# Softmax's division moved from the context to the probabilities, in a three-stage transformer kernel

## The reference, cut to what matters

```
scores = einsum('bhqd,bhkd->bhqk', q / sqrt(32), k) + attention_bias      # 8 x 16 x 512 x 512
scores = where(src_mask, -inf, scores)
probs  = softmax(scores, axis=-1)
ctx    = einsum('bhqk,bhkd->bhqd', probs, v)                              # then reshaped to B, S, D
x      = x + (ctx @ Wo + bo)
```

## Time and profile before

| | |
|---|---|
| time, median of 3 runs | 2397.74 us (2396.6 to 2398.53) |
| the profiled execution | 2398.12 us, its span 2396.3 us |
| granted TensorE clock, mean | 0.998 |
| busy: TensorE / VectorE / ScalarE / GpSimd | 2362.5 / 1359.5 / 1012.1 / 1019.7 us |
| attention stage, first score to last turn | 794.3 to 1672 us |

### The profile page before, as it was taken

The page is one execution under the profiler, slowest core; times in us unless marked ns, Lnnn a source line. Parts: engine busy times, 40 slices in busy tenths (PEclk is TensorE's granted clock), DMA queues, the critical chain, the costliest instruction groups (busy, mean ns, idle before and its releaser), DMA issues. The chain is left out here.

```text
span 2396.3 us, 42236 instructions
## 1 busy us (share of the span) xinstructions
PE 2362.5 (99%) x16100; PEld 1894.6 (79%) x16100; DVE 1359.5 (57%) x2749; ACT 1012.1 (42%) x2057; POOL 1019.7 (43%) x829
## 2 busy tenths in 40 slices
PE   9999999999999899999999999997999999999999
PEld 7788888888888677777777777775888888888887
DVE  7355464555557777777777777778443333323332
ACT  6132232331332776776767676767311111111111
POOL 0042341432424896767677776767113203203200
PEclk9999999999999999999999999999999999999999
DMA  7110101101122556565656566564320110110100
GB/s 231 42 45 21 44 24 55 44 18 61 44 73 102 161 182 205 168 200 163 212 158 203 170 200 194 169 211 164 123 71 1 53 53 0 53 53 1 51 35 18
DMA packets 142197, 243.94 MB, mean 102 GB/s; under 512 B 14140, under 2 KB 28620, under 8 KB 142048
## 3 DMA queue, kind: packets, MB, share of 16 engines
q1 hardware_dynamic: 141520, 241.66, 31.4%
q10 hardware_dynamic: 528, 0.26, 0.0%
HBM read 216.69 MB, written 25.20 MB: 101 GB/s over the span
## 5 line engine op out<-in xcount | busy, mean ns | idle before, releaser
L1254 POOL TENSOR_TENSOR at_bias<-at_bias,at_mask 128x512 f32<-128x512 f32 x512 | 596.4, 1192 | 231.7 <-DMA at_bias<-in_fside_Bx16xSxS 224.8
L646 ACT ACTIVATE L_hid<-bank,L_b1c 128x512 f32<-128x512 f32 x256 | 176.6, 690 | 962.0 <-PE bank L290 961.8
L845 DVE CAST L_hh<-L_hid 128x512 fp32r<-128x512 f32 x256 | 122.9, 480 | 739.1 <-PE bank L972 710.5
L288 PE MATMUL bank<-xth,L_w1h 128*128 128x512 f32 x1024 | 403.2, 394 | 0.1
L289 PE MATMUL bank<-xth,L_w1l 128*128 128x512 f32 x1024 | 400.0, 391 | 0.0
L290 PE MATMUL bank<-xtl,L_w1h 128*128 128x512 f32 x1024 | 399.7, 390 | 0.0
L970 PE MATMUL bank<-L_w2h,L_hh 128*128 128x512 f32 x1016 | 398.4, 392 | 0.0
L972 PE MATMUL bank<-L_w2l,L_hh 128*128 128x512 f32 x1016 | 396.0, 390 | 0.0
L971 PE MATMUL bank<-L_w2h,L_hl 128*128 128x512 f32 x1016 | 395.8, 390 | 0.0
L1311 ACT ACTIVATE at_bias<-at_bias,cos_sin 128x512 f32<-128x512 f32 x512 | 363.3, 713 | 8.5 <-DVE cos_sin L1452 8.0
L1452 DVE CUSTOM_DVE_ANT_0 at_bias<-bank,at_bias 128x512 f32<-128x512 f32 x512 | 331.3, 684 | 36.6 <-PE bank L1643 24.6
(11 more groups left out here) (213 smaller groups left out, 3240.9 us busy)
## 6 DMA issues: line engine op xcount, KB each, us to landing
at_bias<-in_fside_Bx16xSxS SPq DMA_DIRECT2D x256, 512.0 KB, 3.7
L_xres<-in_x SPq DMA_DIRECT2D x8, 1024.0 KB, 5.3
x_scratch<-L_xres SPq DMA_DIRECT2D x8, 1024.0 KB, 4.3
at_xres<-x_scratch SPq DMA_DIRECT2D x32, 256.0 KB, 4.3
L_xin<-x_scratch SPq DMA_DIRECT2D x8, 1024.0 KB, 5.6
L_xres<-x_scratch SPq DMA_DIRECT2D x8, 1024.0 KB, 5.6
L_ring<-in_L_cond_w SPq DMA_DIRECT2D x31, 256.0 KB, 4.9
L_xin<-in_x SPq DMA_DIRECT2D x7, 1024.0 KB, 5.2
```

Source lines behind the costliest of these rows:

```text
L288: nc_mm = pe.matmul(out, ah, bh, start=i == 0, stop=False)
L646: nc.scalar.activation(hid[m % 2][:, :], turn[m % 2][:, :], func, bias=b1c[:, m:m + 1]).then_inc(h_act, 1)
L1254: nc.gpsimd.tensor_tensor(tile, tile, mask[:, m % TT, :], ALU.add).then_inc(masked, 1)
```

## The change

The division goes to the probabilities: behind the exponentials of a block, VectorE takes the reciprocals of its four sums and multiplies each of the four units in place by its column (`scale`), and TensorE's turn of a unit waits for that (`scaled`) instead of for the exponential. `over`, `over_by`, `normal` and `normalize` go. The two halves of the context are read from `ctx_ps` itself, and the next phase's context waits for the low half. The copy of unit 1 goes from VectorE to ScalarE. VectorE's `inverse` and scales 0 and 1 stand at the head of its turn, scales 2 and 3 behind scores 0 and 1. Its core (semaphore lists and deleted bodies left out):

```diff
@@ scalar
+            done = pt_odd if j % 2 else pt_even
+            nc.scalar.activation(pt[:, j, :, :].rearrange("p k q -> p (k q)"), turn[j % 2][:, :], ACT.Copy).then_inc(done, 1)
...
         def context_hi(b, phase, alone=False):
-            act.wait_ge(normed, b * PHASES + phase + 1)
+            act.wait_ge(pv_mm, b * BLOCKS + TT * phase + TT)
...
-            nc.scalar.activation(cth[:, phase, :], normal[:, :], ACT.Identity, bias=bvc[:, phase:phase + 1]).then_inc(ct_hi, 1)
+            nc.scalar.activation(cth[:, phase, :], ctx_ps[:, :], ACT.Identity, bias=bvc[:, phase:phase + 1]).then_inc(ct_hi, 1)
...
@@ scalar, body
-                if u == 0 and phase:
-                    over(b, phase - 1, first)
-                elif u == 0 and not first:
-                    over(b - 1, PHASES - 1)
...
+                turn_out(b, m, 1, first)
                 if after:
                     exp(*after, 1)
@@ vector
+        def inverse(b, m):
+
+            dve.wait_ge(exped, b * UNITS + GROUP * m + GROUP)
+            nc.vector.reciprocal(inv[:, 0:GROUP], sums[:, GROUP * m:GROUP * m + GROUP]).then_inc(inv_set, 1)
+            dve.wait_ge(inv_set, b * BLOCKS + m + 1)
+
+        def scale(b, m, j):
+            tile = bias[:, (GROUP * m + j) % SLOTS, :]
+            nc.vector.tensor_scalar(tile, tile, inv[:, j:j + 1], None, ALU.mult).then_inc(scaled, 1)
...
-            nc.vector.scalar_tensor_tensor(ctl[:, phase, :], normal[:, :], bvc[:, phase:phase + 1],
+            nc.vector.scalar_tensor_tensor(ctl[:, phase, :], ctx_ps[:, :], bvc[:, phase:phase + 1],
...
@@ vector, body
                 before = m - 1
+                inverse(b, m)
+                scale(b, m, 0)
+                scale(b, m, 1)
...
                 if after:
                     scores(*after, 0)
+                scale(b, m, 2)
+                if after:
                     scores(*after, 1)
-                if u == 0 and phase:
-                    normalize(b, phase - 1)
-                elif u == 0 and not first:
-                    normalize(b - 1, PHASES - 1)
-                if u == TT - 1:
-                    inverse(b, phase, first)
-                turn_out(b, m, 1, first)
+                scale(b, m, 3)
                 if after:
                     scores(*after, 2)
@@ tensor
-                pe.wait_ge(normed, b * PHASES + tile)
+                pe.wait_ge(ct_lo, b * PHASES + tile)
...
-            pe.wait_ge(exped, b * UNITS + n + 1)
+            pe.wait_ge(scaled, b * UNITS + n + 1)
...
-            if j == 0 and m % TT == 0 and not (first and m == 0):
-                pe.wait_ge(over_out, b * PHASES + m // TT)
...
@@ tensor, body
-                if m % TT == TT - 1:
-                    over(b, m // TT)
```

More of the change, by code:

```diff
@@ L1119, in attention_stage @@
     pt = at(HIDDEN, "pt", [P, GROUP, KT, P])
-    over_by, normal = at(PT, "over_by", [P, S]), at(SETUP, "normal", [P, S])
-    spread = normal[:, :].rearrange("p (n d) -> p n d", d=HD)
     neg_top, sums, inv = keep.neg_top, keep.sums, keep.inv
@@ L1134, in attention_stage @@
         "masked", "score_mm", "scored", "exped", "turned", "pt_even", "pt_odd", "pv_mm"))
[L1135 to L1139, removed]
+    x_mm, nat_mm, v_mm, o_mm = map(sem, ("x_mm", "nat_mm", "v_mm", "o_mm"))
+    xt_hi, xt_lo, nat_hi, nat_lo, v_out, o_out = map(sem, ("xt_hi", "xt_lo", "nat_hi", "nat_lo", "v_out", "o_out"))
+    inv_set, scaled, ct_hi, ct_lo, res_ready = map(sem, ("inv_set", "scaled", "ct_hi", "ct_lo", "res_ready"))
     passed_dve, passed_sp = sem("passed_dve"), sem("passed_sp")
@@ L1405, in scalar @@
         each_pair(act, body)
-        over(B - 1, PHASES - 1)
         context_hi(B - 1, PHASES - 1)
@@ L1456, in turn_out @@
             dve.wait_ge(turned, b * UNITS + GROUP * m + j + 1)
-            if j == 1 and not (first and m == 0):
+            if not (first and m == 0):
                 dve.wait_ge(pv_mm, b * BLOCKS + m)
             nc.vector.tensor_copy(pt[:, j, :, :].rearrange("p k q -> p (k q)"), turn[1][:, :]).then_inc(pt_odd, 1)
[L1461 to L1473, removed]
+        def inverse(b, m):
[5 more added lines that the diff above has]
+            nc.vector.tensor_scalar(tile, tile, inv[:, j:j + 1], None, ALU.mult).then_inc(scaled, 1)
         def context_lo(b, phase):
             dve.wait_ge(ct_hi, b * PHASES + phase + 1)
-            nc.vector.scalar_tensor_tensor(ctl[:, phase, :], normal[:, :], bvc[:, phase:phase + 1],
+            nc.vector.scalar_tensor_tensor(ctl[:, phase, :], ctx_ps[:, :], bvc[:, phase:phase + 1],
                                            cth[:, phase, :].bitcast(F32), ALU.add, ALU.subtract).then_inc(ct_lo, 1)
@@ L1572, in vector @@
         each_pair(dve, body)
-        normalize(B - 1, PHASES - 1)
         context_lo(B - 1, PHASES - 1)
@@ L1624, in output @@
                 mm.then_inc(o_mm, 1)
[L1626 to L1631, removed]
         def scores(b, m, first=False):
@@ L1767, in x_ready @@
             pe.wait_ge(xt_lo, x_count(B) + KT)
-            pe.wait_ge(over_out, B * PHASES)
+            pe.wait_ge(ct_lo, B * PHASES)
         each_pair(pe, body)
```

## The result

The changed kernel takes 2587.69 us (median of 4, 2584.6 to 2590.18) against 2397.56 us (4 runs, 2396.6 to 2398.53): ratio 1.0793, 95% interval 1.0781 to 1.0806, which is 190 us more. The forecast was slower, 2520 us, range 2440 to 2620: the direction and the range held, and the loss was half as large again as the point's (190 against 123 us). The profiled execution took 2588.45 us.

A forecast was written before the change was run, and what follows sets the result against it. TensorE bounds the kernel before (6.86 us a block); VectorE was to take over at 6.31 + 1.4 = 7.7 us. 128 x 7.7 + 15 = 1000.6 against 877.7 us adds 123 to 2398.12: 2520 us, range 2440 to 2620.

The forecast's parts named there:

- TensorE's floor: Attention stage: TensorE's own work after the change allows no block shorter than 6.73 us, against 6.86 before.
- the removals: Attention stage: TensorE loses 32 groups of transposes of the reciprocals, 17 us in all; VectorE's removed work is hidden today.
- The loop: VectorE, from one fourth score to the next, through exponential, reciprocal, multiplications and scores: 6.31 us a block without GpSimd waits.
- the port wait: VectorE's four multiplications wait for the SBUF port shared with GpSimd: 1.4 us a block, making it 7.7 us.
- the alternation: At 760 us in the old trace, VectorE and GpSimd took turns: 1.43 us per VectorE instruction instead of 0.685, 0.74 lost.
- The ends: First and last batch of the attention stage: weight splits and statistics on VectorE's path cost an estimated 15 us (0 to 20).
- TensorE stays the bound: Rival for the attention stage: multiplications lose under 0.42 us a block to GpSimd; 2381 us, faster; chance 0.04.
- the small wait: Rival: port waits of only 0.45 to 1.0 us a block, bursts settling apart; 2400 to 2455 us; chance 0.13.
- Full alternation: Rival: all four multiplications take turns with GpSimd, losing 2.97 us; 9.28 us a block, +330 us, 2728; chance 0.08.
- GpSimd becomes the bound: Rival: GpSimd, blocked in turn, needs 6.7 us a block, below VectorE's loop; chance counted within the 0.04 of TensorE staying bound.

The follow-up runs named there:

- the version that runs near TensorE's floor: Changed kernel with multiplications that also sum their row, two reciprocals a block, and unit 3's copy on ScalarE too: 2419.46 us against 2399.68 for the kernel before.

## Why the prediction was right in direction and short in size

**TensorE's floor and the removals.** 17 us from the turned reciprocals was right within 3 to 5 us (12 to 14 measured). ScalarE's added copy, priced at nothing, costs 5 us in the kernel before, where TensorE sets the pace; in the change VectorE does, and what the copy costs there was not measured.

**The loop.** VectorE sets the pace and closes the loop that was laid out. Without the port's price I had 6.31 us a block; measured, 8.28 (600 us for 290 multiplications) less 2.02 of waits is 6.26. The sum came out better than its parts. A multiplication adds 0.40 (1221.29 to 1221.69), not 0.43, which is 0.12 less a block; reciprocal and handoff took 0.21, not 0.30. Against that, the stretch with the copy, the wait for the exponential, the context's low half and the mask took 1.41 us, where I had 1.13 + 0.10: by distances of starts from 900 to 1500 us, the copy adds 0.66 with 0.06 idle before it, the idle time before the reciprocal is 0.37 (0.55 in the block shown), the low half 0.17 and the mask 0.15, which had been given only a part of the 0.10.

**The step that was mis-sized** is the port wait, 1.4 us a block. It measured (0.978 - 0.472) x 4 = 2.02 us, so 0.62 x 128 = 79 us of the loss were missed by it; the mean of a multiplication, forecast as 0.7 to 0.8 us, was 0.978. The forecast took for three of the four the mean of what the stage's SBUF instructions lost before, 0.30, and the alternation's 0.74 x 0.71 for one. But those instructions of before stood at other places in the block. The additions come in bursts, and their start is tied by the loads to TensorE's turns, hence to VectorE's own multiplications: three of four fell into the burst. By their place in the block, the four took 1.020, 1.224, 1.051 and 0.615 us on average (900 to 1500 us), so they waited 0.55, 0.75, 0.58 and 0.14, where I had 0.30, 0.53, 0.30 and 0.30. That GpSimd is busy 63% of the time now (442.9 of 700 us) says nothing about the chance of meeting it. The runs show the coupling: moving the multiplications changed the mean wait. Why this phase is the one into which the kernel settles was not taken apart.

**The ends** were charged 15 us on top of 128 blocks. 128 x 8.28 = 1060 us against the 1066.9 of the stage's window: 7 us, though some 25 us in the version that runs near TensorE's floor. The account closes: 128 x (8.28 - 7.7) = 74 us more in the loop (79 from the port, 5 or 6 less from the other parts) and 8 less at the ends give 123 + 74 - 8 = 189 us. That the point missed by 67 us and not by 79 was the luck of the small terms.

**The rivals.** "TensorE stays the bound" needed the multiplications to lose under 0.42 us a block together, the small wait 0.45 to 1.0; they lost 2.0. The bursts are tied to the turns, as that rival said, but they settled on the multiplications and not beside them. Full alternation needed 2.97 (by its own sum 128 x 9.28 + 15 = 1202.8 us, +325 and 2723, not +330 and 2728); the second multiplication paid its price (0.75 against 0.74), the fourth often went free. "GpSimd becomes the bound" did not happen: it stood idle for loads 348.7 us in all (224.8 before).

## What to carry to other kernels

Before putting SBUF-to-SBUF work on VectorE beside a busy GpSimd, price the wait for each instruction and not the work: here it was 0.5 us each, the same for 2 columns as for 512, and the form that takes 0.74 us instead of 0.47 but does not contend made the kernel 128 us faster. A mean wait taken from other places of a block is no estimate for a new place, because both engines' bursts hang on the same semaphores. And work put at the head of an in-order queue delays all that stands behind it, which here were the low halves and outputs that TensorE waited for as long as for the multiplications.

## What the runs showed of the hardware

A two-column TENSOR_SCALAR on VectorE took 0.214 us when free and up to 1.344 us beside GpSimd's 1.15 us additions. The same multiplication with a row sum took 0.736 to 0.751 us beside the same additions, the plain one 0.472 to 1.516. The granted clock of TensorE was 0.97 of the full 2.4 GHz over the changed stage, where TensorE was idle 15% of the time, against 1.00 before; since VectorE set the pace there, I read no cost from it.
